# A sandwich layer on one core: the high and low halves of the non-convolution weights are kept in DRAM and loaded as pairs

## The chip, the core and the metric

The kernel runs on one core of one Trainium2 chip. Its engines work side by side and meet through semaphores: TensorE (PE) multiplies, VectorE (DVE), ScalarE (ACT) and GpSimd (POOL) work on tiles in SBUF, and SyncE (SP) issues the transfers between DRAM and SBUF. The metric is the device time in microseconds (us) of one execution; lower is better. It is given as the median of several runs.

## What is computed

The input is 4 sequences of 512 tokens with 1024 features, all in float32. Each passes through an attention block and a small mixture of experts, both wrapped in layer norms and residual sums:

```
h   = layernorm(x)
c   = conv1d(h, conv_w[3, 1024, 768], 'SAME') + conv_b        # q, k, v: 256 columns each
q,k,v = split(c);  qh = q@wq + bq;  kh = k@wk + bk;  vh = v@wv + bv   # 256 -> 16 heads of 64
p   = softmax(causal(qh @ kh.T / 8))                          # in blocks of 128 tokens
o   = (p @ vh) @ wo + bo                                      # 1024 -> 256
x1  = x + layernorm(o @ proj_w + proj_b)                      # 256 -> 1024
t   = layernorm(x1)
g   = softmax of the two largest of t @ Wr.T (4 experts), others 0
out = x1 + layernorm(sum over e of g[e] * 4 * (t @ A[e].T) @ B[e].T)   # rank 16
```

## The kernel before

**Products in two halves.** A float32 product is made of three products in a reduced float32 format: each operand is the sum of a high half (its rounded copy) and a low half (the rest), and `mm3` adds high*high, high*low and low*high. So every weight needs a high and a low copy. The weights come in 304 chunks of at most 128x512 numbers, listed in order of use in `CHUNKS`. Five kinds exist: `conv` (48 in each of the four batches), `v` (4 in a batch), `qk` (8), `wo` (8, only 256 wide) and `proj` (8, which are 4 different chunks used by two pairs of token tiles). For each chunk SP loads the float32 numbers into one of 6 slots `raw`, ACT rounds them into one of 6 slots `w_hi` (L931), and POOL or DVE subtracts to get `w_lo` (L1342, L1137). All non-convolution chunks have their low half made on POOL. The same weights are loaded and split again in every batch.

**Order of work.** The class `Plan` writes out one list of stages for all engines. Each engine's program walks the list in order and does the stages that concern it, and waits on semaphores for what it needs; so a wait holds up everything behind it on the same engine, and on SP too. Splits are planned 5 chunks ahead of their use (`LEAD`), and a load as soon as its raw slot's earlier chunk has been split, which is up to 6 chunks earlier still. A split of chunk k on ACT waits until PE has used chunk k-6, whose slot it takes.

**One batch.** The convolution comes first, in six turns of 8 chunks (a three-tap convolution done as four filters on half the tokens). In batches 1 to 3 its slots carry side work for the batch before (`SIDE`): output projection with the `proj` chunks at slots 9 to 11, layer norm 2, layer norm 3, the experts, layer norm 4 and the store of the result at slots 38 and 43. Behind each store, `load_x` brings the input of the batch after next into the same tiles `work`; it waits until the store has landed. Then come `project_v` (first half of the columns for four token tiles, then the second half), and a loop over pairs of heads: `project_qk`, `scores`, softmax, transposes, `attend`, `project_wo`. Eight convolution chunks of the next batch fill its last three rounds. `load_residual` follows the loop: the four input tiles again, 512 KB each. After batch 3 comes `TAIL`, the same side work with little to hide behind.

**Names that the prediction uses.** `work` are the four input tiles; DVE takes their statistics at L1074 and L1075 (`x_stats`), and the first layer norm needs all four. `std` is a chain of 13 small DVE instructions (L1062 to L1070), each waiting for the one before, which gives 1/standard deviation by Newton steps. `conv_out` and `conv_add` (POOL L1349, DVE L1159 and L1162) put the filters together; `project_qk` of the first pair waits for the last of them. `k_t` (DVE L1176) is the key copy that `scores` (PE L810) waits for. POOL also adds the residuals (L1362 in layer norm 2, L1368 in layer norm 4).

Of the kernel before, what the change touches and what calls it, by code (L numbers as in the profile page):

```python
# [4 lines left out]
F32 = mybir.dt.float32  # L5
I32 = mybir.dt.int32
F32R = mybir.dt.float32r
# [115 lines left out]


SUMMED = [k for k, name in enumerate(CHUNKS) if is_summed(name)]
LOADED = [k for k, name in enumerate(CHUNKS) if not is_summed(name)]

# [10 lines left out]
class Plan:  # L138
# [42 lines left out]
    def load_chunks(self):  # L181
        while self.loaded < len(CHUNKS):
            k = self.loaded
            name = CHUNKS[k]
            if not is_summed(name):
                n = LOADED.index(k)
                if n >= RAW_SLOTS and ("split", LOADED[n - RAW_SLOTS]) not in self.known:
                    break
                first = name[:2] == ("conv", 0) and name[3:] == (0, 0)
                if first and name[2] != C_ORDER[0]:  # L190
                    before = C_ORDER[C_ORDER.index(name[2]) - 1]
                    if ("sum", NUMBER["conv", 0, before, 3, HALVES - 1]) not in self.known:
                        break
                self.put("load", k)
                if first:
                    self.put("load_tap1", name[2])
            self.loaded += 1

    def split_chunks(self, upto):
# [5 lines left out]
        while self.split <= min(upto, len(CHUNKS) - 1):  # L205
# [3 lines left out]
            self.split += 1  # L209
            self.put("split", k)  # L210
            self.load_chunks()

    def use_chunk(self, *name, over=True):
# [271 lines left out]
def build(nc, x, conv_w, wq, wk, wv, wo, proj_w, biases, proj_b, aw, b_t, out):  # L485
    with ExitStack() as ctx:
# [15 lines left out]
        raw_slots = [sb(f"raw{i}", [P, CHUNK]) for i in range(RAW_SLOTS)]  # L502
        w_hi = [sb(f"w_hi{i}", [P, CHUNK], F32R) for i in range(SPLIT_SLOTS)]
        w_lo = [sb(f"w_lo{i}", [P, CHUNK], F32R) for i in range(SPLIT_SLOTS)]
        xt = [sb(f"xt{i}", [P, L + 2]) for i in range(2)]
# [51 lines left out]

        summed = nc.dram_tensor("summed_filters", (NC, 2, HALVES, P, CHUNK), F32, kind="Internal").ap()

        plan = Plan()  # L560
# [114 lines left out]
        s_tap1 = [sem(f"s_tap1_{h}") for h in range(HALVES)]  # L675
        s_small, s_lora = sem("s_small"), sem("s_lora")
        raw_full, sum_kept, work_full, stored, tap1_full = Arrival(), Arrival(), Arrival(), Arrival(), Arrival()
        for stage, *a in stages:
            if stage == "load":
                for _ in range(2 if CHUNKS[a[0]][0] == "qk" else 1):  # L680
# [32 lines left out]
        def tensor_program(pe):  # L713
# [12 lines left out]
            def use_chunk(*name):  # L726
                k = NUMBER[name]
                w.wait_ge(*split_high(k))
                w.wait_ge(*split_low(k))
                return k, w_hi[k % SPLIT_SLOTS], w_lo[k % SPLIT_SLOTS]  # L730
# [165 lines left out]
        def scalar_program(act):  # L896
# [29 lines left out]
            def split(k):  # L926
                n = width_of(k)
                if k >= SPLIT_SLOTS:
                    w.wait_ge(*chunk_used(k - SPLIT_SLOTS))
                w.wait_ge(*raw_ready(k))  # L930
                act.activation(w_hi[k % SPLIT_SLOTS][:, 0:n], raw_of(k)[:, 0:n], ACT.Copy).then_inc(*split_high.now(k))  # L931
# [446 lines left out]
        def sync_program(sp):  # L1378
# [5 lines left out]
            def tap_half(tap, c, half):  # L1384
                rows = slice(half * HALF * P, (half + 1) * HALF * P)
                return conv_w[tap, rows, c * P:(c + 1) * P].rearrange("(k p) n -> p k n", p=P)

            def load(k):
                name = CHUNKS[k]
                n = LOADED.index(k)  # L1390
                slot, full = raw_slots[n % RAW_SLOTS], s_raw[n % RAW_SLOTS]
# [63 lines left out]
            def store(b, t0):  # L1455
# [4 lines left out]
            run = {  # L1460
                "load": load, "load_tap1": load_tap1, "sum": sum_, "load_x": load_x, "load_residual": load_residual,
                "setup": setup, "store": store,
# [43 lines left out]
```

## Time and profile before

| | us |
|---|---|
| median of 3 runs | 950.44 (947.37 to 952.57) |
| the profiled execution, its own time | 947.76 |
| its span, from first to last instruction | 946.0 |
| PE, PEld busy | 776.5, 687.6 |
| DVE, POOL, ACT busy | 688.2, 526.1, 494.1 |
| mean granted clock of TensorE | 0.913 of full speed |
| bytes read, written in DRAM | 90.47 MB, 14.68 MB |

Times in the trace count from the first instruction. Batch 0 takes the first 220 us or so, the batches repeat every 218 to 219 us, and the tail begins at about 860. An engine's busy time is the sum of its instructions; PE instructions overlap, so a busy PE is not a PE at its peak. The granted clock is 1.00 at 2.4 GHz and 0.50 at 1.2 GHz.

### The profile page before, as it was taken

To read this page: it belongs to the slowest core of one execution; us is meant where nothing else is said; L and a number is where in the kernel's file an instruction comes from. 1 tells how busy PE (TensorE), PEld (TensorE's weight loads), DVE (VectorE), ACT (ScalarE), POOL (GpSimd) and SP (SyncE) were. 2 spreads that over 40 slices of the span, in tenths; PEclk is the share of its full clock that TensorE was granted. 3 is DMA by queue.
4 is the path that set the end of the run, shared out by engine and by line. 5 is a ranking of instruction groups with operands and counts; after the bars stand their busy time and mean duration, and the time that the engine had idled before them with its cause. 6 is when DMAs were issued, how large, how long until landed. Compare 5 with 4: busy or idle time off the path is not lost.

```text
span 946.0 us, 15442 instructions
## 1 busy us (share of the span) xinstructions
PE 776.5 (82%) x5136; PEld 687.6 (73%) x5136; DVE 688.2 (73%) x1796; ACT 494.1 (52%) x1156; POOL 526.1 (56%) x450
## 2 busy tenths in 40 slices
PE   2587788999949697999968887999986968997573
PEld 1487786888949685788968776788886967876472
DVE  6988777895887665987696675798597673555856
ACT  3443346875436345676536445777436445565332
POOL 2555574667673573676773564677783456444211
PEclk9889999999979897999988987999997979999856
DMA  7254662113724262212733345111743433113002
GB/s 212 74 157 129 209 208 76 40 57 98 248 68 146 80 226 85 57 45 81 247 109 106 118 149 164 45 52 51 236 143 90 125 119 125 49 53 123 1 0 89
DMA packets 108414, 106.15 MB, mean 112 GB/s; under 512 B 7600, under 2 KB 83376, under 8 KB 108336
## 3 DMA queue, kind: packets, MB, share of 16 engines
q1 hardware_dynamic: 108336, 105.18, 35.4%
q8 instruction: 41, 0.67, 0.3%
q14 instruction: 37, 0.30, 0.1%
HBM read 90.47 MB, written 14.68 MB: 111 GB/s over the span
## 4 chain that ended last, share of the span: by engine, by line
DVE 39%; PE 36%; ACT 9%; issue 9%; DMA 5%; POOL 1%; SPq 0%; DVEq 0%; ACTq 0%
PE bank L733 9%; PE bank L734 8%; PE bank L735 8%; ACT prob L981 5%; PE bank L867 3%; DVE newton L1067 3%; DVE prob_t L1200 3%; DVE filt L1097 2%; PE bank L810 2%; DVE newton L1068 2%; DVE ln_r L1069 2%; DVE ln_r L1065 2%; PE bank L829 2%; DVE prob L1184 2%; DMA work<-x 2%
## 5 line engine op out<-in xcount | busy, mean ns | idle before, releaser
L1342 POOL TENSOR_TENSOR w_lo<-raw,w_hi 128x512 fp32r<-128x512 f32 (+1 forms) x217 | 271.5, 1265 | 142.7 <-ACT w_hi L931 141.0
L733 PE MATMUL bank<-f_hi,w_hi 128*128 128x256 f32 x768 | 232.0, 302 | 40.2 <-POOL w_lo L1342 19.7
L734 PE MATMUL bank<-f_lo,w_hi 128*128 128x256 f32 x768 | 225.3, 293 | 0.0
L735 PE MATMUL bank<-f_hi,w_lo 128*128 128x256 f32 x768 | 224.8, 293 | 0.0
L931 ACT ACTIVATE w_hi<-raw 128x512 fp32r<-128x512 f32 (+1 forms) x280 | 162.0, 600 | 70.4 <-PE bank L735 59.3
L733 PEld LDWEIGHTS bank<-f_hi,w_hi 128*128 128x128 f32 x768 | 156.0, 203 | 47.2 <-ACT w_hi L931 19.1
L734 PEld LDWEIGHTS bank<-f_lo,w_hi 128*128 128x128 f32 x768 | 155.9, 203 | 0.8
L735 PEld LDWEIGHTS bank<-f_hi,w_lo 128*128 128x128 f32 x768 | 155.5, 202 | 0.0
L1353 POOL TENSOR_TENSOR prob<-prob,rtotal 128x512 f32<-128x512 f32 x64 | 84.4, 1331 | 123.4 <-DVE rtotal L1192 123.4
L981 ACT ACTIVATE prob<-prob,ntop 128x128 f32<-128x128 f32 x256 | 99.3, 390 | 36.5 <-DVE ntop L1188 36.5
L1137 DVE TENSOR_TENSOR w_lo<-raw,w_hi 128x512 fp32r<-128x512 f32 x63 | 55.9, 895 | 16.8 <-ACT w_hi L931 16.8
L733 PE MATMUL bank<-c_hi,w_hi 128*128 128x512 f32 x128 | 57.3, 448 | 8.1 <-DVE prob L1162 6.2
L810 PE MATMUL bank<-k_t,q_t 64*128 64x128 f32 x512 | 55.9, 289 | 8.3 <-DVE k_t L1176 8.2
L1184 DVE CUSTOM_DVE_ANT_0 prob<-bank,mask 128x128 f32<-128x128 f32 x256 | 58.4, 281 | 3.6 <-PE bank L810 3.5
L810 PEld LDWEIGHTS bank<-k_t,q_t 64*128 64x128 f32 x512 | 49.9, 191 | 14.9 <-issue 14.9
L860 PE MATMUL bank<-ident,v 128*128 128x128 f32 x128 | 23.0, 340 | 42.2 <-ACT v L902 42.2
L1368 POOL TENSOR_TENSOR work<-work,v 128x1024 f32<-128x1024 f32 x14 | 35.1, 2530 | 39.9 <-ACT v L902 39.7
L924 ACT ACTIVATE f_hi<-filt 128x1024 fp32r<-128x1024 f32 x28 | 29.6, 1058 | 51.1 <-POOL filt L1335 48.4
L1349 POOL TENSOR_TENSOR k_t<-q_t 128x256 f32<-128x256 f32 x48 | 38.0, 813 | 30.7 <-ACT q_t L948 26.0
L829 PE MATMUL bank<-prob_t,v 128*64 128x128 f32 x512 | 51.9, 279 | 2.9 <-DVE prob_t L1200 2.9
L1362 POOL TENSOR_TENSOR work<-work,v 128x1024 f32<-128x1024 f32 x14 | 33.8, 2433 | 34.1 <-ACT v L902 34.1
L734 PE MATMUL bank<-c_lo,w_hi 128*128 128x512 f32 x128 | 51.7, 404 | 0.0
(132 smaller groups left out, 1739.7 us busy)
## 6 DMA issues: line engine op xcount, KB each, us to landing
raw<-conv_w SPq DMA_DIRECT2D x96, 256.0 KB, 3.1
raw<-summed_filters SPq DMA_DIRECT2D x72, 256.0 KB, 2.8
work<-x SPq DMA_DIRECT2D x32, 512.0 KB, 5.6
raw<-proj_w SPq DMA_DIRECT2D x32, 256.0 KB, 2.9
out<-work SPq DMA_DIRECT2D x16, 512.0 KB, 3.8
summed_filters<-prob_t SPq DMA_DIRECT2D x16, 256.0 KB, 4.3
raw<-wv SPq DMA_DIRECT2D x16, 256.0 KB, 3.0
raw<-wq SPq DMA_DIRECT2D x32, 128.0 KB, 2.3
```

Of the source, the lines that this page charges most:

```text
L733: pe.matmul(dst, w_h, m_h, start=start, stop=False)
L734: pe.matmul(dst, w_h, m_l, start=False, stop=False)
L735: return pe.matmul(dst, w_l, m_h, start=False, stop=stop)
L810: ins = pe.matmul(score_banks[g][:, toks], q_t[rows, toks], k_t[rows, toks], start=True, stop=True)
L829: ins = pe.matmul(acc[g * DH:(g + 1) * DH, toks], v[:, t, head:head + DH], prob_t[:, g, toks], start=True, stop=True)
L931: act.activation(w_hi[k % SPLIT_SLOTS][:, 0:n], raw_of(k)[:, 0:n], ACT.Copy).then_inc(*split_high.now(k))
L981: ins = act.activation(prob[:, g, t, :], prob[:, g, t, :], ACT.Exp, bias=ntop[:, g, t:t + 1], scale=QK_SCALE, accum_out=total[:, g, t:t + 1])
L1137: dve.tensor_tensor(lo, raw_of(k)[:, 0:n], hi.bitcast(F32), ALU.subtract).then_inc(*split_low_dve.now(k))
L1184: ins = dve.tensor_tensor_reduce(prob[:, g, t, :], score_banks[g][:, t * P:(t + 1) * P], mask[:, :], 1.0, NEG_INF * 4, ALU.add, ALU.max, t ...
L1342: pool.tensor_tensor(lo, raw_of(k)[:, 0:n], hi.bitcast(F32), ALU.subtract).then_inc(*split_low_pool.now(k))
L1349: pool.tensor_tensor(m12_sums[:, i, :], m12[:, 0, :], m12[:, 1, :], op).then_inc(*m12_summed.now(b, turn, i))
L1353: pool.tensor_tensor(prob[:, g, :, :], prob[:, g, :, :], rtotal[:, g, :].rearrange("p (t o) -> p t o", o=1).broadcast_to([P, TB, P]), ALU. ...
```

## The change

The first chunk with given weights (all of batch 0's `v`, `qk` and `wo`, and the first four `proj`: 24 chunks in all, `KEPT`) is loaded and split as before, and then SP also writes its high and low half, side by side, to a DRAM tensor `kept_pairs` (stage `keep`). In batches 1 to 3 the 84 non-convolution chunks (`is_whole`) are no longer loaded as float32 and split: one transfer of both halves, 512 KB (256 KB for `wo`), goes straight into the slot `w_pair` (`load_whole`). It needs no raw slot, but it needs the slot of chunk k-6 free, so SP itself waits for the use of chunk k-6, and the load is planned when chunk k-5 is used. Raw slots now serve the convolution, batch 0 and the last four `proj` of batch 0 alone. The loads stay in one order, so a convolution load behind a whole one waits with it.

```diff
--- before.py
+++ after.py
@@ -122,8 +122,22 @@
     return name[0] == "conv" and name[1] == 0 and name[3] in (1, 2)
 
 
+def weights_of(name):
+    return name[:1] + (name[3:] if name[0] == "proj" else name[2:])
+
+
+def is_whole(k):
+    return CHUNKS[k][0] != "conv" and CHUNKS[k][1] > 0
+
+
 SUMMED = [k for k, name in enumerate(CHUNKS) if is_summed(name)]
-LOADED = [k for k, name in enumerate(CHUNKS) if not is_summed(name)]
+WHOLE = [k for k in range(len(CHUNKS)) if is_whole(k)]
+LOADED = [k for k, name in enumerate(CHUNKS) if not is_summed(name) and not is_whole(k)]
+KEPT = {}
+for k, name in enumerate(CHUNKS):
+    if name[0] != "conv":
+        KEPT.setdefault(weights_of(name), k)
+KEPT_AT = {weights: i for i, weights in enumerate(KEPT)}
 
 
 def low_on_dve(k):
@@ -182,7 +196,11 @@
         while self.loaded < len(CHUNKS):
             k = self.loaded
             name = CHUNKS[k]
-            if not is_summed(name):
+            if is_whole(k):
+                if ("used", k - SPLIT_SLOTS) not in self.known:
+                    break
+                self.put("load", k)
+            elif not is_summed(name):
                 n = LOADED.index(k)
                 if n >= RAW_SLOTS and ("split", LOADED[n - RAW_SLOTS]) not in self.known:
                     break
@@ -207,8 +225,11 @@
             if k >= SPLIT_SLOTS and ("used", k - SPLIT_SLOTS) not in self.known:
                 break
             self.split += 1
-            self.put("split", k)
+            if not is_whole(k):
+                self.put("split", k)
             self.load_chunks()
+            if k in KEPT.values():
+                self.put("keep", k)
 
     def use_chunk(self, *name, over=True):
         k = NUMBER[name]
@@ -500,8 +521,8 @@
         aw_sb = sb("aw_sb", [P, KD, ER + E])
         lora_b = [sb(f"lora_b{i}", [P, D], F32R) for i in range(2)]
         raw_slots = [sb(f"raw{i}", [P, CHUNK]) for i in range(RAW_SLOTS)]
-        w_hi = [sb(f"w_hi{i}", [P, CHUNK], F32R) for i in range(SPLIT_SLOTS)]
-        w_lo = [sb(f"w_lo{i}", [P, CHUNK], F32R) for i in range(SPLIT_SLOTS)]
+        w_pair = [sb(f"w_pair{i}", [P, 2, CHUNK], F32R) for i in range(SPLIT_SLOTS)]
+        w_hi, w_lo = [pair[:, 0, :] for pair in w_pair], [pair[:, 1, :] for pair in w_pair]
         xt = [sb(f"xt{i}", [P, L + 2]) for i in range(2)]
         filt = sb("filt", [P, FILT, L2])
         f_hi = sb("f_hi", [P, KD, FILT, L2], F32R)
@@ -556,6 +577,8 @@
         banks_of = {"stream": bank[0:2], "v": bank[2:4], "turn": bank[4:6], "side": bank[6:8]}
 
         summed = nc.dram_tensor("summed_filters", (NC, 2, HALVES, P, CHUNK), F32, kind="Internal").ap()
+
+        kept_pairs = nc.dram_tensor("kept_pairs", (len(KEPT), P, 2, CHUNK), F32, kind="Internal").ap()
 
         plan = Plan()
         stages, at = plan.stages, plan.at
@@ -674,9 +697,16 @@
         s_out = [sem(f"s_out{t}") for t in range(TB)]
         s_tap1 = [sem(f"s_tap1_{h}") for h in range(HALVES)]
         s_small, s_lora = sem("s_small"), sem("s_lora")
+        s_whole = [sem(f"s_whole{i}") for i in range(SPLIT_SLOTS)]
+        s_kept = [sem(f"s_kept{i}") for i in range(SPLIT_SLOTS)]
         raw_full, sum_kept, work_full, stored, tap1_full = Arrival(), Arrival(), Arrival(), Arrival(), Arrival()
+        whole_full, pair_kept = Arrival(), Arrival()
         for stage, *a in stages:
-            if stage == "load":
+            if stage == "load" and is_whole(a[0]):
+                whole_full.expect(s_whole[a[0] % SPLIT_SLOTS], a[0])
+            elif stage == "keep":
+                pair_kept.expect(s_kept[a[0] % SPLIT_SLOTS], a[0])
+            elif stage == "load":
                 for _ in range(2 if CHUNKS[a[0]][0] == "qk" else 1):
                     raw_full.expect(s_raw[LOADED.index(a[0]) % RAW_SLOTS], a[0])
             elif stage == "load_tap1":
@@ -725,8 +755,11 @@
 
             def use_chunk(*name):
                 k = NUMBER[name]
-                w.wait_ge(*split_high(k))
-                w.wait_ge(*split_low(k))
+                if is_whole(k):
+                    w.wait_ge(*whole_full(k))
+                else:
+                    w.wait_ge(*split_high(k))
+                    w.wait_ge(*split_low(k))
                 return k, w_hi[k % SPLIT_SLOTS], w_lo[k % SPLIT_SLOTS]
 
             def mm3(dst, w_h, w_l, m_h, m_l, start, stop):
@@ -927,6 +960,8 @@
                 n = width_of(k)
                 if k >= SPLIT_SLOTS:
                     w.wait_ge(*chunk_used(k - SPLIT_SLOTS))
+                if k - SPLIT_SLOTS in KEPT.values():
+                    w.wait_ge(*pair_kept(k - SPLIT_SLOTS))
                 w.wait_ge(*raw_ready(k))
                 act.activation(w_hi[k % SPLIT_SLOTS][:, 0:n], raw_of(k)[:, 0:n], ACT.Copy).then_inc(*split_high.now(k))
 
@@ -1385,8 +1420,24 @@
                 rows = slice(half * HALF * P, (half + 1) * HALF * P)
                 return conv_w[tap, rows, c * P:(c + 1) * P].rearrange("(k p) n -> p k n", p=P)
 
+            def load_whole(k):
+                i, n, first = k % SPLIT_SLOTS, width_of(k), KEPT[weights_of(CHUNKS[k])]
+                w.wait_ge(*chunk_used(k - SPLIT_SLOTS))
+                if k - SPLIT_SLOTS in KEPT.values():
+                    w.wait_ge(*pair_kept(k - SPLIT_SLOTS))
+                w.wait_ge(*pair_kept(first))
+                sp.dma_start(w_pair[i][:, :, 0:n].bitcast(F32), kept_pairs[KEPT_AT[weights_of(CHUNKS[k])], :, :, 0:n]).then_inc(s_whole[i], 16)
+
+            def keep(k):
+                i, n = k % SPLIT_SLOTS, width_of(k)
+                w.wait_ge(*split_high(k))
+                w.wait_ge(*split_low(k))
+                sp.dma_start(kept_pairs[KEPT_AT[weights_of(CHUNKS[k])], :, :, 0:n], w_pair[i][:, :, 0:n].bitcast(F32)).then_inc(s_kept[i], 16)
+
             def load(k):
                 name = CHUNKS[k]
+                if is_whole(k):
+                    return load_whole(k)
                 n = LOADED.index(k)
                 slot, full = raw_slots[n % RAW_SLOTS], s_raw[n % RAW_SLOTS]
                 if n >= RAW_SLOTS:
@@ -1458,7 +1509,7 @@
                     sp.dma_start(out[b * TB + t], work[t][:, :]).then_inc(s_out[t], 16)
 
             run = {
-                "load": load, "load_tap1": load_tap1, "sum": sum_, "load_x": load_x, "load_residual": load_residual,
+                "load": load, "keep": keep, "load_tap1": load_tap1, "sum": sum_, "load_x": load_x, "load_residual": load_residual,
                 "setup": setup, "store": store,
             }
             for stage, *args in stages:
```

## Rows read from the trace of the kernel before

**Rows 1.** The page, its first part: busy us, share of the span, instructions.
```profile
PE 776.5 (82%) x5136; PEld 687.6 (73%) x5136; DVE 688.2 (73%) x1796; ACT 494.1 (52%) x1156; POOL 526.1 (56%) x450
```

**Rows 2.** Stretches: us, busy PE, PEld, DVE, ACT, POOL, then clock, DMA share, GB/s.
```profile
394.50:403.43 8.93, 8.93 (x63) 7.39 (x63) 8.11 (x28) 6.70 (x23) 6.36 (x6) 1.00 0.20 59
...
474.00:548.00 74.00, 53.35 (x413) 52.29 (x412) 58.13 (x137) 34.26 (x55) 40.19 (x29) 0.87 0.35 104
```

**Rows 3.** Groups by line and shape, the two splits.
```profile
L1342 POOL TENSOR_TENSOR w_lo<-raw,w_hi 128x512 fp32r<-128x512 f32 x185 | 245.5, 1339 | 140.6 <-ACT w_hi L931 138.9
...
L931 ACT ACTIVATE w_hi<-raw 128x512 fp32r<-128x512 f32 x248 | 150.0, 625 | 70.4 <-PE bank L735 59.3 <-DMA raw<-proj_w 7.5 <-DMA raw<-wk 1.5
...
L1342 POOL TENSOR_TENSOR w_lo<-raw,w_hi 128x256 fp32r<-128x256 f32 x32 | 26.7, 837 | 2.1 <-ACT w_hi L931 2.1
```

**Rows 4.** Timeline (start, us, instruction, idle before) around batch 1's `project_v`.
```profile
347.83 0.35 PE L733 MATMUL bank<-f_hi,w_hi 128*128 128x256 f32 x1 [1.08 <-DVE w_lo L1137]
...
360.38 0.79 PE L733 MATMUL bank<-c_hi,w_hi 128*128 128x512 f32 x1 [3.66 <-DVE prob L1162]
...
367.04 1.68 PE L810 MATMUL bank<-k_t,q_t 64*128 64x128 f32 x16 [1.30 <-DVE k_t L1176]
...
341.63 5.50 POOL L1368 TENSOR_TENSOR work<-work,v 128x1024 f32<-128x1024 f32 x2 [2.56 <-ACT v L902]
...
358.26 0.69 DVE L1074 BATCH_NORM_STATS2 stats<-work 128x6 f32<-128x512 f32 x1 [8.19 <-DMA work<-x]
...
348.69 0.93 SPq L1458 DMA_DIRECT2D out<-work  x2
```

**Rows 5.** The chain that ended last, 348 to 359 (start, us, what).
```profile
348.69 3.16 DMA out<-work
351.87 6.38 DMA work<-x
```

**Rows 6.** Busy time by stretch, batch 1's `project_v` and `project_qk`.
```profile
349.30:356.60 7.30, 7.30 (x32) 5.40 (x30) 0.77 (x2) 2.34 (x4) 7.17 (x7) 1.00 1.01 332
356.60:360.30 3.70, 0.12 (x1) 0.00 (x0) 2.04 (x4) 0.00 (x0) 0.00 (x0) 0.77 0.83 268
360.30:366.00 5.70, 5.36 (x12) 3.79 (x12) 4.14 (x19) 3.60 (x7) 1.97 (x2) 0.55 0.23 69
```

**Rows 7.** Timeline, batch 3: the same place.
```profile
778.01 5.51 POOL L1368 TENSOR_TENSOR work<-work,v 128x1024 f32<-128x1024 f32 x2 [2.36 <-ACT v L902]
...
785.71 0.39 PE L733 MATMUL bank<-w_hi,c_hi 128*128 128x512 f32 x1
```

**Rows 8.** Timeline, batch 0: the same place.
```profile
135.32 1.26 SPq L1440 DMA_DIRECT2D work<-x  x1
...
140.13 0.69 DVE L1074 BATCH_NORM_STATS2 stats<-work 128x6 f32<-128x512 f32 x1 [3.64 <-DMA work<-x]
...
143.50 0.69 DVE L1074 BATCH_NORM_STATS2 stats<-work 128x6 f32<-128x512 f32 x1
...
148.93 1.23 PE L810 MATMUL bank<-k_t,q_t 64*128 64x128 f32 x12 [3.65 <-DVE k_t L1176]
```

**Rows 9.** Busy time by stretch: output projection, and residual loads alone.
```profile
446.00:476.00 30.00, 30.00 (x205) 27.55 (x206) 20.15 (x33) 14.01 (x23) 20.56 (x17) 1.00 0.77 245
...
467.00:470.00 3.00, 3.00 (x21) 2.67 (x20) 2.65 (x5) 1.90 (x3) 1.30 (x2) 1.00 1.00 362
...
864.00:867.00 3.00, 1.80 (x9) 1.51 (x10) 1.11 (x3) 3.00 (x14) 1.18 (x2) 1.00 0.99 396
```

**Rows 10.** Timeline, side work of batch 1: POOL's splits and layer norm 2.
```profile
472.56 1.21 DVE L1067 TENSOR_TENSOR newton<-ln_r 128x2 f32<-128x2 f32 x1
475.24 0.16 DVE L1067 TENSOR_TENSOR newton<-ln_r 128x2 f32<-128x2 f32 x1
...
468.69 6.30 POOL L1342 TENSOR_TENSOR w_lo<-raw,w_hi 128x512 fp32r<-128x512 f32 x5 [2.66 <-ACT w_hi L931]
...
457.43 2.25 SPq L1445 DMA_DIRECT2D work<-x  x4
```

## The prediction

> **What bounds the kernel now.** I read the page first: PE is busy for 82% of the span and every other engine for less [rows 1]. Then the busy time by stretch, to see where PE is not full. In the steady rounds of attention it is full: 8.93 of 8.93 us at clock 1.00, while ACT has 6.70 us of work and POOL 6.36 [rows 2]. So an ACT or POOL instruction taken out there is worth nothing. PE's slack lies behind the output projection: 53.35 busy in 74.00 us [rows 2], where it waits for the layer norms. Last I read the timeline and the chain at the start of the projections of batches 1 to 3, because there a store, a load and `project_v` meet. PE waits 3.66 us for the last filter sum and 1.30 us for `k_t` [rows 4], and its clock drops to 0.55 [rows 6].
>
> **What is removed.** 84 loads and splits. On POOL that is 60 x 1.339 + 24 x 0.837 = 100 us, on ACT at least 60 x 0.625 = 37 us [rows 3]. Nearly all of it runs under a full PE, so I count it as nothing there. If PE were not the cover, an attention round would be set by DVE (8.11 us), which loses no instruction.
>
> **What is added.** The 60 wide pairs carry 0.262 MB more each, the 24 narrow ones 0.131, together 18.9 MB; the 24 kept pairs are 10.5 MB of writes. At 396 GB/s [rows 9] a pair of 0.524 MB takes 1.32 us of the DMA engines. A store of that size that went out alone landed 3.16 us after its issue [rows 5], so I take 3.16 for a transfer alone and 1.32 more for each in front of it. The real question is what is late, stretch by stretch.
>
> **Batches 1 and 2, start of the projections.** Before, all loads of `v` were out long in advance. Now the load of the first `v` chunk is planned at the use of chunk k-5, which is slot 43, behind the store of tiles 2 and 3. SP waits there for POOL's residual sum, done at 341.63 + 5.50 = 347.13 [rows 4]. So: store of tile 3 at 347.2, first `v` pair at 347.6, here at 347.2 + 3.16 + 1.32 = 351.7. Then `load_x` of tile 2 needs its store landed (stored at 344.4 when the first of the two sums is done, landed 347.6), goes out at 348.0, and the second `v` pair at 348.4 lands at 351.7 + 2 x 1.32 = 354.3. Queued behind are `load_x` of tile 3 (its store lands at 350.4), the second half of `v` and the first `qk` pair, each 1.3 us apart, so 355.6 to 359.5. PE is ready for `v` at about 349.3 and does 30 products at 0.228 us [rows 6]: three at 351.7, 27 from 354.3, done at 360.5. Before, `project_qk` began at 360.38 [rows 4], because DVE stood 8.19 us for tile 2, a load issued at 351.87 behind a store issued at 348.69 [rows 4, 5]. In the new order tile 2 goes out at 348.0, nearly 4 us sooner, and the filter sums are ready before 356. So `project_qk` starts at the same time; what limited it was the input tile, and what limits it now is the `v` pair. The gain is behind it: the fourth tile's statistics and `std` no longer hold `k_t`, so the 1.30 us wait goes, and about 0.7 us of slow clock with it. I take -2 us for each. The unknown is TensorE's clock, since 4.4 us of waits now lie before 30 products instead of before 12. If these run at half speed, 30 x 0.228 = 6.8 us is added and the 2.6 us that the low clock took from 12 products returns: +2 with the gain. If the clock doesn't fall at all: -5.
>
> **Batch 3, the same place.** There is no next input, and PE goes from the convolution straight into `v` at 785.71 [rows 7]; nothing hides a late pair. POOL ends at 778.01 + 5.51 = 783.52, the store goes at 783.6, the first pair lands at 783.6 + 3.16 + 1.32 = 788.1, the second at 789.4. Three products fit between. So 27 products start at 789.4 instead of 785.71 + 0.7: +3.0 us. Bounds: +1 if the pairs do not queue, +6 if the clock falls for the products behind.
>
> **Batch 0, the same place.** Pairs of `v` are being written while the input of batch 1 comes in. The third tile's load, at 135.32, gets one kept pair in front (+1.3), the fourth two (+2.6). DVE takes the third at once when it comes (140.13, after a wait of 3.64) and the fourth at 143.50, and `k_t` keeps PE waiting 3.65 us at 148.93 [rows 8]. The fourth has about 0.7 us of slack (an estimate): +1.9 us. Bounds 0 and 2.6.
>
> **Output projection of batches 1 and 2.** Eight pairs instead of eight single chunks: 2.1 MB more in a stretch of 30 us in which the DMA engines are 77% busy, and full for its middle third, at 362 GB/s [rows 9]. 2.1 MB are 5.3 us of them, of 6.9 us free. But the 2.1 MB of residuals, issued at 457.43 [rows 10], now go out two `proj` pairs earlier, in front of the fourth pair, which then is about 1 us late; the convolution chunk behind it, loaded later and still to be split, 1 us more. Against that POOL no longer has two of the five low halves under `std`: four DVE steps take 1.21 us instead of 0.16 while POOL works [rows 10], but the three convolution splits left move into the same place, so one step is won. +2 - 1 = +1 us for each, passed on because the layer norms set this stretch. Bounds -4 (all four steps fast) and +6. In batch 0 the four `proj` pairs written cost the last loads some 4 us; layer norm work on DVE covers about that, and the 20.65 us that PE idles behind it [rows 2] cover the rest: +0.5, bounds 0 and 4.
>
> The Trainium skill (HBM Reference, its bandwidth table and the text below it) puts a core that streams alone at about 425 GB/s, and at 358 when both cores of a pair do. By the second figure a pair would take 1.46 us (an estimate from that page), the sum grows by under 2 us. The trace agrees with the first: 396 GB/s in long rows.
>
> **Elsewhere.** In the attention rounds a pair is asked for five chunks ahead, which is over two rounds of 8.93 us: covered. In the tail the `proj` pairs are there before the last head is done: nothing.
>
> **Sum.** +1.9 + 0.5 - 2 - 2 + 1 + 1 + 3.0 = +3.4 us on the profiled execution's own 947.76, so 951.2. That execution lies 2.7 us under the median of the runs shown, 950.44; on the median the sum gives 953.8. I take 953.0, nearer to the median.
>
> **Rivals.** *Relief counts (faster).* POOL's two-input work holds DVE up: 1.21 against 0.16 us. If four steps are freed in both output projections (-8) and the clock stays up in front of `project_qk` (-10), with batches 0 and 3 as above (+5.4), it is -13: about 938. With half of that, 944. It decides when at least two steps a batch are freed and the `v` pairs land before 353. The Trainium skill (GPSIMD Engine Reference, Specifications) says that GpSimd shares its SBUF interfaces with VectorE; the slow steps agree with that. Against: the slow steps lie under convolution splits, which stay.
> *Late pairs (slower).* In the output projection the DMA engines are already full where the pairs come. If each pair costs its 1.32 us on PE's path from the fourth on, that is +6 in each of two, +2 in batches 1 and 2, +6 in batch 3 and +6 in batch 0: +28, about 979; half of it, 965, is likelier. For it: SP now stops at the store. Against: 6.9 us of free DMA time.
> *No effect.* PE-bound and all transfers hidden: 950. It isn't told apart from my forecast by time.
>
> **How the numbers follow.** My forecast, with no effect in it, has a chance of 0.43, relief 0.27, late pairs 0.30. A change under 0.5% (4.8 us) can't be told from none. 953.0 is +0.3%. For its own case the range is 947 to 957; relief reaches to 938 and late pairs to 979, and leaving a tenth at each end gives 941 to 969. Faster by more than 0.5% is the larger part of relief and nothing else, 0.27; slower takes late pairs, 0.30, and the top of my case, 0.02, from the same, 0.41.
>
> **What would show it.** In the profile after: POOL some 100 us and ACT 40 to 50 us less busy; about 135 MB moved; attention rounds still 8.9 us; PE waiting for transfers of pairs at the start of `project_v` in batches 1 to 3, for 2 to 5 us each; `load_x` of tile 2 issued within 1 us of POOL's last sum; DMA share of 0.9 or more in the output projection. I am wrong if PE waits for pairs in attention, if the low clock covers more stretches than before, or if `std` in layer norm 2 runs through without a step over 1 us.

## The result, and the profile after

The kernel became slower: 978.36 us median of 4 runs (977.12 to 981.14), against 948.90 (947.20 to 952.57) for the kernel before in the same rounds. The ratio is 1.032, 95% interval 1.0297 to 1.0343. The profiled execution spans 976.0 us, before 946.0. The time lies outside the ranges around the forecast of 953.0 (947 to 957 for its own case, 941 to 969 with the rivals); the rival "late pairs", with 979, comes nearest.

The page of the kernel after: busy us of each engine, bytes, and the transfers (KB each, us from issue to landing).

```profile
span 976.0 us, 15110 instructions
PE 781.1 (80%) x5136; PEld 691.9 (71%) x5136; DVE 685.0 (70%) x1796; ACT 454.6 (47%) x1072; POOL 430.7 (44%) x366
...
DMA packets 106364, 135.50 MB, mean 139 GB/s; under 512 B 7600, under 2 KB 76208, under 8 KB 106288
...
w_pair<-kept_pairs SPq DMA_DIRECT2D x60, 512.0 KB, 4.6
```

Against [rows 1], POOL has 95.4 us less work (526.1 to 430.7) and ACT 39.5 us less. So the change does what it says, and none of it shortens the time. PE is busy 781.1 us instead of 776.5 with the same 5136 products, and its mean granted clock is 0.903 instead of 0.913; it stands for the rest of the span, 194.9 us instead of 169.5. So 25.4 of the 30.0 us are standing.

**Where the 30 us are.** I take three marks on PE in every batch: the first `scores` (S), the first turn of the experts' input (T), and the turn behind the gates of the second pair of token tiles (M). S to T holds the attention rounds, the output projection and the layer norms in front of the experts; M to S the end of the convolution, the store, `project_v` and the first `project_qk`. All times in us, from one profiled execution of each kernel; "to S, batch 0" counts from the first instruction. The marks are read to about 0.1 us.

| stretch | before | after | forecast of the difference | measured |
|---|---|---|---|---|
| to S, batch 0 | 148.9 | 153.0 | +1.9 | +4.1 |
| S to M behind batch 0's attention | 180.4 | 181.6 | +0.5 | +1.2 |
| M to S, start of batch 1's attention | 37.7 | 37.3 | -2 | -0.4 |
| S to M, batch 1's output projection in it | 180.5 | 190.9 | +1 | +10.4 |
| M to S, batch 2's | 36.8 | 37.6 | -2 | +0.8 |
| S to M, batch 2's output projection in it | 181.3 | 190.9 | +1 | +9.6 |
| M to S, batch 3's | 31.2 | 35.5 | +3.0 | +4.3 |
| behind S of batch 3, the tail in it | 149.2 | 149.2 | 0 | 0.0 |

The measured column adds up to 30.0, the difference of the spans. Two thirds of it are in the output projections of batches 1 and 2.

**What happens there.** The timeline of batch 1's output projection in the kernel after, engine by engine (start, us, instruction, and in brackets the idle time before it with what ended it):

```profile
455.68 3.14 SPq L1429 DMA_DIRECT2D w_pair<-kept_pairs  x3
458.88 2.25 SPq L1496 DMA_DIRECT2D work<-x  x4
461.22 0.61 SPq L1429 DMA_DIRECT2D w_pair<-kept_pairs  x1
461.93 0.81 SPq L1456 DMA_DIRECT2D raw<-conv_w  x1
...
471.80 0.63 ACT L966 ACTIVATE w_pair<-raw 128x512 fp32r<-128x512 f32 x1 [11.28 <-DMA raw<-conv_w]
...
472.46 0.69 DVE L1172 TENSOR_TENSOR w_pair<-raw,w_pair 128x512 fp32r<-128x512 f32 x1 [9.91 <-ACT w_pair L966]
473.07 0.68 DVE L1254 TENSOR_TENSOR v<-bank,projb 128x512 f32<-128x512 f32 x1
...
473.81 0.79 PE L766 MATMUL bank<-w_pair,po_hi 128*128 128x512 f32 x1 [8.33 <-DVE v L1254]
...
702.14 0.80 PE L766 MATMUL bank<-w_pair,po_hi 128*128 128x512 f32 x1 [8.49 <-DVE v L1254]
```

Read it from the end. PE stands 8.33 us because DVE has not emptied a bank of the output projection (`proj_bias`, L1254). DVE is idle, though; it walks its list in order, and in front of that instruction stands the low half (L1172) of a convolution chunk, slot 10 of the next batch. For that DVE needs ACT's high half, and ACT stands 11.28 us for the chunk itself. The load of the chunk went out at 461.93 and was there at 471.7. The last row is the same place in batch 2. The chain that ended last goes the same way (start, us, what):

```profile
461.93 9.78 DMA raw<-conv_w
...
471.80 0.64 ACT w_pair L966
...
473.07 0.70 DVE v L1254
...
473.81 0.79 PE bank L766
```

Why a chunk of 256 KB takes 9.78 us is seen in SP's waits between 446 and 470 (us in total, times, longest), and in the busy time by stretch (columns as in [rows 2]):

```profile
SPq L1429 <- PE bank L768: 12.2, 4, 9.1
```

```profile
446.00:450.00 4.00, 3.14 (x22) 2.58 (x21) 1.81 (x3) 1.00 (x2) 1.46 (x2) 1.00 0.95 311
450.00:453.00 3.00, 3.00 (x29) 2.83 (x28) 1.04 (x3) 1.60 (x4) 1.27 (x1) 1.00 0.04 12
453.00:456.00 3.00, 3.00 (x22) 2.72 (x21) 0.40 (x1) 1.45 (x3) 2.29 (x2) 1.00 0.00 0
...
465.00:468.00 3.00, 0.48 (x3) 0.05 (x1) 0.00 (x0) 0.00 (x0) 0.00 (x0) 1.00 1.03 416
468.00:471.00 3.00, 0.00 (x0) 0.00 (x0) 0.00 (x0) 0.00 (x0) 0.00 (x0) 0.74 1.06 383
471.00:474.00 3.00, 0.19 (x1) 0.20 (x2) 1.51 (x3) 0.63 (x1) 0.00 (x0) 0.50 0.83 301
474.00:477.00 3.00, 3.00 (x8) 2.32 (x9) 2.63 (x5) 1.15 (x2) 0.00 (x0) 0.50 0.04 11
477.00:480.00 3.00, 3.00 (x12) 2.52 (x11) 1.83 (x3) 0.00 (x0) 0.00 (x0) 0.56 0.32 106
...
455.68:471.71 16.03, 9.80 (x72) 8.94 (x70) 2.38 (x4) 1.87 (x3) 2.04 (x3) 0.93 0.89 319
```

From 450 to 455.7 nothing moves (share 0.04 and 0.00). SP stands at the load of a pair, which may not go before PE has used chunk k-6; one such wait is 9.1 us long. Then three pairs, the four residuals, one more pair and the chunk go out within 7 us. They are 4.5 MB; with the first part of two more pairs behind them the DMA engines move 5.1 MB in the 16.03 us until the chunk is there, at 319 GB/s.

From 465.5 to 473.8 PE does nothing, and then it works at clock 0.50 (1.2 GHz) until about 479.7. A product starts every 0.43 us there, later every 0.23, so the 5.9 us of work at the low clock cost some 2.7 us (an estimate from these rows). The stall and this make 11.0, a little more than the 10.4 of the table, because the kernel before has a low clock elsewhere in the stretch (0.50 from 368.9 to 372.2, right behind S, where this kernel has 1.00). Over S to T as a whole PE stands 24.9 us instead of 15.1 and is busy 119.2 instead of 118.5.

**The start of the projections** in batch 1, SP and PE:

```profile
349.51 3.15 SPq L1509 DMA_DIRECT2D out<-work  x2
352.76 0.38 SPq L1429 DMA_DIRECT2D w_pair<-kept_pairs  x1
353.18 0.78 SPq L1491 DMA_DIRECT2D work<-x  x1
354.06 0.41 SPq L1429 DMA_DIRECT2D w_pair<-kept_pairs  x1
...
357.41 0.77 PE L766 MATMUL bank<-w_pair,c_hi 128*128 128x512 f32 x1 [2.78 <-issue]
359.92 0.80 PE L766 MATMUL bank<-w_pair,c_hi 128*128 128x512 f32 x1 [0.89 <-DMA w_pair<-kept_pairs]
...
371.88 1.68 PE L843 MATMUL bank<-k_t,q_t 64*128 64x128 f32 x16 [0.93 <-DVE k_t L1211]
```

Everything is about 5 us later than in [rows 4], since batch 0 has cost that much. The order is as forecast: the store, the first `v` pair, the input tile 0.4 us behind it, the second pair. PE waits for the pairs, and the 3.66 us before `project_qk` are gone. (The profile names no releaser for the 2.78 us; they are gone where `v` is loaded as before, in a run below.) But the stretch is as long as before: 2.78 and 0.89 us are as much as the 3.66, `k_t` still keeps PE for 0.93 us where it was 1.30, and the clock falls to 0.50 for 6.8 us in both kernels, here behind 356.8 and before behind 358.6.

### The profile page after: what moved, and what is told of

It reads as the page before. It is cut to its first block, busy times and chain, and to the rows that moved or that the text cites. A ratio compares the mean times of both kernels' runs of the same rounds, so it can differ in the third digit from the quotient of the medians.

```text
span 976.0 us, 15110 instructions
## 1 busy us (share of the span) xinstructions
PE 781.1 (80%) x5136; PEld 691.9 (71%) x5136; DVE 685.0 (70%) x1796; ACT 454.6 (47%) x1072; POOL 430.7 (44%) x366
## 4 chain that ended last, share of the span: by engine, by line
PE 40%; DVE 34%; issue 8%; DMA 7%; ACT 7%; SPq 2%; POOL 2%; ACTq 0%; DVEq 0%; POOLq 0%
PE bank L766 10%; PE bank L768 9%; PE bank L767 9%; ACT prob L1016 3%; PE bank L843 3%; PE bank L862 3%; PE bank L900 3%; DVE newton L1102 3%; DVE ln_r L1104 2%; DVE newton L1103 2%; DMA raw<-conv_w 2%; DVE ln_r L1100 2%; DVE prob_t L1235 2%; PE bank L893 2%; DVE stats L1321 2%
## 5 line engine op out<-in xcount | busy, mean ns | idle before, releaser
L766 PE MATMUL bank<-f_hi,w_pair 128*128 128x256 f32 x768 | 231.6, 302 | 37.5 <-POOL w_pair L1377 17.5
L1377 POOL TENSOR_TENSOR w_pair<-raw,w_pair 128x512 fp32r<-128x512 f32 (+1 forms) x133 | 172.9, 1312 | 168.6 <-ACT w_pair L966 167.6
L767 PE MATMUL bank<-f_lo,w_pair 128*128 128x256 f32 x768 | 225.1, 293 | 0.0
L768 PE MATMUL bank<-f_hi,w_pair 128*128 128x256 f32 x768 | 224.9, 293 | 0.0
L766 PEld LDWEIGHTS bank<-f_hi,w_pair 128*128 128x128 f32 x768 | 156.0, 203 | 44.4 <-issue 16.5
L966 ACT ACTIVATE w_pair<-raw 128x512 fp32r<-128x512 f32 (+1 forms) x196 | 116.6, 615 | 97.3 <-PE bank L768 38.2
L767 PEld LDWEIGHTS bank<-f_lo,w_pair 128*128 128x128 f32 x768 | 155.8, 203 | 1.0
L768 PEld LDWEIGHTS bank<-f_hi,w_pair 128*128 128x128 f32 x768 | 155.3, 202 | 0.0
L1172 DVE TENSOR_TENSOR w_pair<-raw,w_pair 128x512 fp32r<-128x512 f32 x63 | 54.3, 869 | 40.7 <-ACT w_pair L966 40.7
L766 PE MATMUL bank<-c_hi,w_pair 128*128 128x512 f32 x128 | 54.7, 427 | 4.5 <-DVE prob L1197 2.7
L893 PEld LDWEIGHTS bank<-ident,v 128*128 128x128 f32 x128 | 19.4, 181 | 43.7 <-ACT v L935 43.7
```

Source lines behind the costliest of these rows:

```text
L766: pe.matmul(dst, w_h, m_h, start=start, stop=False)
L767: pe.matmul(dst, w_h, m_l, start=False, stop=False)
L768: return pe.matmul(dst, w_l, m_h, start=False, stop=stop)
L893: ins = pe.transpose(dst[:, i * P:(i + 1) * P], y[t][:, kt * P:(kt + 1) * P], ident[:, :])
L1172: dve.tensor_tensor(lo, raw_of(k)[:, 0:n], hi.bitcast(F32), ALU.subtract).then_inc(*split_low_dve.now(k))
L1377: pool.tensor_tensor(lo, raw_of(k)[:, 0:n], hi.bitcast(F32), ALU.subtract).then_inc(*split_low_pool.now(k))
```

## The experiments

Twelve kernels were run, each compared with the kernel before in the same rounds. None of them leaves out a part of the computation. The stretches come from one profiled execution of each.

### All pairs but those of the output projection

```diff
-    return CHUNKS[k][0] != "conv" and CHUNKS[k][1] > 0
+    return CHUNKS[k][0] in ('v', 'qk', 'wo') and CHUNKS[k][1] > 0
...
-    if name[0] != "conv":
+    if name[0] in ('v', 'qk', 'wo'):
```

> The changed kernel with the proj chunks loaded and split as before; v, qk and wo stay kept pairs. Theory A (the loss sits in the output projection, where the pairs and the 2 MB of residual loads stand in one queue in front of convolution chunk 158, whose low half on DVE stands in front of the bias additions): the two waits of 8.3 and 8.5 us and the slow clock behind them go, 978 - 25 = 953 us. Theory B (each of the 84 pairs costs about the same wherever it is loaded): 24 of 84 pairs gone is 0.3 of 30 us, 969 us. Theory C (the writes and the first stretches of batch 0 cost most): above 970 us.

Measured: 953.14 us (951.36 to 955.25), ratio 1.0052 (1.0034 to 1.0071), as theory A expected. S to T in batches 1 and 2 takes 131.4 and 131.6 us: not only are the 10 us gone, both are 2 us shorter than before (133.6, 134.0). M to S of batch 3 keeps its extra, 36.8.

### The pairs of the output projection alone

The same two lines with `('proj',)`.

> The opposite: only the proj chunks are kept pairs. Theory A: before + 25, 974 us, with the same two waits of PE of about 8 us at the second half of the output projection. Theory B: before + 9, 958 us. Theory C: under 955 us, for only four pairs are written, and late in batch 0.

Measured: 971.95 us (970.61 to 972.62), ratio 1.0242 (1.0214 to 1.0269), near the 974 of theory A. Its PE rows:

```profile
473.81 0.80 PE L766 MATMUL bank<-w_pair,po_hi 128*128 128x512 f32 x1 [8.56 <-DVE v L1254]
...
701.70 0.80 PE L766 MATMUL bank<-w_pair,po_hi 128*128 128x512 f32 x1 [8.30 <-DVE v L1254]
```

The two halves of the change cost 4.4 and 23.2 us over the kernel before; together 27.6 of the 29.5 of the whole. So the large loss belongs to these eight pairs a batch, whatever the other weights do.

### The residual loads sooner

The four `load_residual` of batches 0 to 2 move from behind the loop over the heads to the start of its round 8 (the ninth), ahead of the pairs of the output projection.

```diff
             for i in range(HP + LAG):
+                if more and i == HP:
+                    for t in range(TB):
+                        put("load_residual", b, t)
...
             put("finish_wo", b)
-            for t in range(TB):
-                put("load_residual", b, t)
+            if not more:
+                for t in range(TB):
+                    put("load_residual", b, t)
```

> The changed kernel; the residual loads of batches 0 to 2 go out one stage earlier, at the start of the ninth round of attention, when the DMA engines stand still, instead of behind the last round. Nothing else is changed. Theory A: chunk 158 no longer stands behind 2.1 MB, it comes 5 us or more earlier, PE's waits of 8.3 and 8.5 us fall under 3, and the clock stays up: 978 - 20 = 958 us. Theory B (the pairs are late in themselves, 2.1 MB more in a full stretch): the waits keep over 5 us each, 972 us or more.

Measured: 962.13 us (961.34 to 962.21), ratio 1.0138 (1.0116 to 1.0159): 16 us of the 29.5 are back, where theory A had 20. S to M is 8.7 and 6.8 us shorter than in the kernel after in batches 1 and 2, so nearly all of it is there. In the timeline the convolution chunk now stands right behind the four pairs, and ACT begins on it 5.2 us after its issue. PE's wait for `proj_bias` is 2.04 us, in batch 2 2.5 us:

```profile
453.81 4.56 SPq L1433 DMA_DIRECT2D w_pair<-kept_pairs  x4
458.46 0.39 SPq L1460 DMA_DIRECT2D raw<-conv_w  x1
...
463.64 0.63 ACT L970 ACTIVATE w_pair<-raw 128x512 fp32r<-128x512 f32 x1 [4.99 <-PE bank L772]
...
465.65 0.50 PE L770 MATMUL bank<-w_pair,po_hi 128*128 128x512 f32 x1 [2.04 <-DVE v L1258]
```

2.1 MB in front of the chunk, at the 416 GB/s of the stretch above, are 5 us. So most of the wait was one for the queue and not for the transfer of that chunk. The same edit also gives 7 us without any pairs (below); how much of the 16 us is that gain was not taken apart.

### The low halves of slots 10 and 11 on POOL

```diff
-LOW_ON_DVE = {5, 7, 10, 11, 16,
+LOW_ON_DVE = {5, 7, 16,
```

> The changed kernel; the low halves of slots 10 and 11 (chunks 158 and 161 and their like in batches 1 to 3) are made on POOL instead of DVE. Theory A with DVE's order as the whole cause: the bias additions no longer wait for chunk 158, PE goes on to project the second half, and the 8 us fall to 3 or less in each of two batches: about 964 us. Theory A with the late load as the cause: PE goes on for 2.8 us and then waits for chunk 158 itself, 3 us less in each: about 971 us. If the fourth proj pair is what PE waits for, nothing changes: 978 us.

Measured: 972.42 us (970.11 to 975.22), ratio 1.0249 (1.0219 to 1.0279), 6 us less than the kernel after. Nothing stands in front of `proj_bias` now, and the wait shrinks from 8.33 and 8.49 us to these:

```profile
470.88 0.55 PE L766 MATMUL bank<-w_pair,po_hi 128*128 128x512 f32 x1 [4.36 <-DMA w_pair<-kept_pairs]
...
694.62 0.80 PE L766 MATMUL bank<-w_pair,po_hi 128*128 128x512 f32 x1 [4.85 <-DMA w_pair<-kept_pairs]
```

So about half of the stall was the order on DVE, and the other half is there without it: the fourth pair itself is late, behind the residuals. That is the cause of the third case expected, which had put the time at 978, with no gain; the time is near the 971 of the second, whose cause (PE waiting for the chunk) does not appear. S to M is 5.3 and 3.7 us shorter than in the kernel after in batches 1 and 2, but M to S of batches 1 and 3 is some 2 us longer. The way through DVE is shown, and so is its limit.

### The residual loads sooner in the kernel before

The edit of the residual loads, in the kernel without pairs.

> The kernel before, with nothing kept, and the residual loads of batches 0 to 2 at the start of the ninth round of attention as in the run of that name. Theory: before the change PE never waited in the output projection, so there is nothing to win: 948 us, within 2 us. Rival: the full queue already cost there (ACT waits 7.5 us for proj loads), 944 us or less.

Measured: 940.82 us (940.14 to 941.93), ratio 0.993 (0.9904 to 0.9956). I had expected no change; the rival was right in time. The gain is spread: 2.6 us in M to S of batch 1, about 1 each in S to T of batches 0 and 2 and in M to S of batch 3. It is not in the output projection of batch 1, where PE is as full as before. And it is not a wait that is gone: over the span PE stands 173.1 us, before 169.5, but is busy 766.6 us with the same 5136 products, before 776.5. M to S of batch 1, before and with the edit (columns as in [rows 2]):

```profile
329.30:367.00 37.70, 31.67 (x172) 27.34 (x172) 22.16 (x54) 16.49 (x29) 20.78 (x16) 0.84 0.58 195
```

```profile
328.70:363.80 35.10, 28.97 (x172) 25.49 (x173) 22.17 (x54) 16.41 (x29) 20.81 (x16) 0.93 0.63 210
```

PE stands 6.0 and 6.1 us; what differs is the granted clock, 0.84 and 0.93. So in these two executions the gain is a higher clock. Why it is higher stays open, and one of the four runs, at a mean clock of 0.912, took 941.93 us all the same, while the kernel before had 0.909 to 0.917 in these rounds.

### All pairs but those of `v`

The two lines with `('qk', 'wo', 'proj')`.

> The changed kernel with the v chunks loaded and split as before; qk, wo and proj stay kept pairs. Theory: at the start of the projections the v pair, whose load stands behind the store on SP, is what PE waits for, and the input tile that used to hold PE now comes early. Without v pairs both waits are gone: batch 3 gains 4.4 us, batches 1 and 2 some 4 us each, batch 0 (four pairs less to write) 2 us: 964 us, with no wait of PE over 1.5 us between the last convolution chunk and the first scores. Rival (the earlier load of the input tile came from the splits that are gone, and is lost with v's splits back): batches 1 and 2 fall back by 2 us each, 976 us.

Measured: 958.45 us (956.54 to 959.08), ratio 1.0114 (1.0091 to 1.0137), more of a gain than expected (964). M to S falls to 31.8 and 31.6 us in batches 1 and 2, from 37.3 and 37.6, and to 31.2 in batch 3. In batch 1 PE stands 2.8 us instead of 5.7 and is busy 29.0 instead of 31.6, so half of the gain is waits and half is clock (0.92 instead of 0.84). The stalls of the output projection are still there, 8.55 and 8.30 us. SP around the store of batch 1:

```profile
348.12 3.15 SPq L1509 DMA_DIRECT2D out<-work  x2
351.31 2.84 SPq L1491 DMA_DIRECT2D work<-x  x2
354.26 5.44 SPq L1429 DMA_DIRECT2D w_pair<-kept_pairs  x4
```

`v` was loaded long before, as single chunks, and the input tiles go out in front of all pairs. So, with the other kinds as pairs, the pairs of `v` cost 5.5 and 6.0 us in batches 1 and 2 (I had this place as a gain of 2) and 4.3 in batch 3.

### The last store later

In front of batch 3 the store of tiles 2 and 3 comes four slots after its place instead of one.

```diff
-            self.later(STORE_LAG, lambda: self.put("store", b, t0))
+            self.later(4 if (b, t0) == (2, 2) else STORE_LAG, lambda: self.put("store", b, t0))
```

> The changed kernel; in the convolution of batch 3 alone the second store of batch 2's result is planned three slots later, so that the loads of the v pairs go out in front of it and not behind it. Theory: SP's stop at the store is what makes the pair late; PE's wait of 2.95 us at batch 3's v goes, with the slow clock behind it 3 to 4 us in all: 974 us. Rival (the pair is late by the time it takes): the wait stays, 978 us.

Measured: 972.70 us (972.02 to 975.13), ratio 1.0272 (1.0247 to 1.0297), near the 974 expected. M to S of batch 3 is 31.0 instead of 35.5; all else is within 1.1 us of the kernel after. The profile had put that wait down to DVE (2.95 us, `prob` L1197), but it goes when only the order of the store and the pairs changes.

### The writes alone

`is_whole` returns `False`: the 24 pairs are written in batch 0 and never read.

> The 24 pairs are written to DRAM in batch 0, and nothing is read back: batches 1 to 3 load and split as before. This prices the writes. Theory: they hold up the input tiles of batch 1, batch 0 is 4 us longer (PE's first scores at about 152 instead of 149 us, and 1 us in the output projection), and nothing else changes: 953 us. Rival (hidden): 949 us. Rival (the rest of batch 0's 5.3 us is the writes in the output projection): over 955 us.

Measured: 951.35 us (949.07 to 953.59), ratio 1.0047 (1.0028 to 1.0067). That is 2.7 to 6.4 us over the kernel before; the median lies between the 953 expected and the 949 of "hidden", nearer to the first. In its profiled execution batch 0's S is at 153.3, where the kernel after has 153.0. But this mark moves without any writes too: in the four kernels that write no pair in front of it, it lies at 148.9 (the kernel before), 149.8, 151.2 and 152.5. So the median prices the writes, and a single timeline does not.

### Pairs of `qk` and `wo` alone

The two lines with `('qk', 'wo')`: what the runs so far left of the change.

> Kept pairs for qk and wo alone: v and proj are loaded and split as before. The stretches of the earlier runs should add up. From scores to scores: with v split as before the start of the projections is 5.9 and 5.1 us shorter than before the change (batches 1 and 2), with proj split as before attention and output projection are 2.1 and 2.5 us shorter, batch 0 gets nothing from writes of v. Theory: 948 - 15 = 933 us. Rival (the gains belong to v and proj pairs, which are gone here): 948 us, as before.

Measured: 932.84 us (931.72 to 934.57), ratio 0.9847 (0.9818 to 0.9876). It is as expected and beats both kernels. M to S is 32.0 and 30.6 us in batches 1 and 2, and S to T is 1.6 and 2.7 us shorter than before. Its SP, to be read against [rows 4, 5]:

```profile
346.18 3.15 SPq L1509 DMA_DIRECT2D out<-work  x2
349.38 2.84 SPq L1491 DMA_DIRECT2D work<-x  x2
352.32 5.45 SPq L1429 DMA_DIRECT2D w_pair<-kept_pairs  x4
```

The input tile is asked for at 349.38, before at 351.87 (though M of batch 0 is 1.7 us later here), and `project_qk` need not wait 3.66 us for the sums behind it. Over the span PE stands 165.8 us instead of 169.5, and is busy 765.5 instead of 776.5 with the same products. So most of this gain too is clock: the waits that are gone are the smaller part of it.

### Pairs of `qk` and `wo`, and the residual loads sooner

> The same with the residual loads of batches 0 to 2 at the start of the ninth round of attention. In the kernel before that gave 7 us. Theory: some of it is in the same waits that the qk pairs have removed, so 2 to 5 us are left: 929 to 931 us. Rival (independent, the full 7 us): 926 us.

Measured: 928.97 us (927.59 to 931.74), ratio 0.9814 (0.9779 to 0.9849). It is as expected and the fastest version of this study, though its slowest run (931.74) touches the fastest of the one above (931.72).

### The store sooner in the kernel before

Is the gain of that version only the earlier store? In the kernel before, the store of tiles 2 and 3 of batches 0 and 1 is put in the plan at once, ahead of the `qk` loads.

```diff
-            self.later(STORE_LAG, lambda: self.put("store", b, t0))
+            if (b, t0) in ((0, 2), (1, 2)):
+                self.put("store", b, t0)
+            else:
+                self.later(STORE_LAG, lambda: self.put("store", b, t0))
```

> The kernel before, with no kept pair; in the convolutions of batches 1 and 2 the second store is planned one slot sooner, in front of the load of the qk chunk that on SP waits for the last split. Theory (the pairs of qk gain at the start of the projections because SP gets sooner to the store and so to the input tile behind it): PE's wait of 3.7 us before project_qk shrinks by 3 us in batch 1 and 2 us in batch 2, with the slow clock behind it 942 us. Rival (the gain comes from the splits that are gone from ACT and POOL): no change, 948 us.

Measured: 941.75 us (940.23 to 948.31, 10 runs), ratio 0.9943 (0.9922 to 0.9964), as expected. M to S: 33.7 and 34.5 us, against 37.7 and 36.8. So part of the gain is a matter of order and needs no pairs. The input tile went out at 354.57, still behind loads of `qk`.

### Pairs of `qk` alone

> Kept pairs for qk alone. Theory (the gain is SP's: the loads behind the last convolution chunks that stop it at a split are those of qk): nearly all of the gain of qk and wo together, within 3 us of that run, 934 to 936 us. Rival (the gain is in the number of splits taken off POOL and ACT, 24 of 48 here): half of it, 941 us.

Measured: 937.31 us (935.50 to 938.24), ratio 0.989 (0.9861 to 0.9919). It lies between what was expected and the rival's 941. M to S is nearly as short as with `wo` (31.4, 32.4), so these 10.9 us under the kernel before are the pairs of `qk`, and the other 4.5 come with those of `wo`, in S to T of batch 2 above all (134.2 against 131.3). There PE stands 14.8 us here and 15.5 with the pairs of `wo`, but is busy 119.4 and 115.8 with the same products, at clock 0.95 and 0.97: again clock and not a wait. Why was not taken apart.

## Why the prediction was wrong, step by step

- **What is removed is worth nothing under a full PE:** right. From 372 to 446 PE is busy 71.71 us at clock 1.00, before 71.77; POOL has 39.45 us of work there instead of 52.45.
- **Output projection of batches 1 and 2, the step that failed: the cost of late loads, taken as +1 each.** The prediction said "2.1 MB are 5.3 us of them, of 6.9 us free", "about 1 us late; the convolution chunk behind it [...] 1 us more", and so +1 each. Measured: +10.4 and +9.6. Two things in it were wrong. The free time of the DMA engines was an average over 30 us, but the change itself moves the start of every load: 5.7 us of it lie before 455.7, when SP may not issue. (What this stop costs by itself no run shows.) And the late chunk was priced at its own use, but it is waited for sooner: its low half is made on DVE, in front of the instruction that empties PE's banks. The fourth pair was taken to be 1 us late; without the low half in front PE waits 4.4 and 4.9 us for it. The same pairs without the other weights cost 23.2 us; with the residuals out of the way 16 us come back; without the low half on DVE half of each stall stays. So the queue behind SP's stop is shown as the cause, with two ways to PE, one through DVE and one through the fourth pair.
- **Start of batches 1 and 2, -2 each:** the waits came as described (5.1 us later, the store, the pairs and the input tile go out within 0.6 us of the times forecast), the gain did not: -0.4 and +0.8. The step that failed here is "the 1.30 us wait goes, and about 0.7 us of slow clock with it": in batch 1 `k_t` keeps PE for 0.93 us and the low clock lasts 6.8 us as before. In batch 2 PE stands 5.7 us instead of 6.0 and is busy 31.9 instead of 30.8. Taking the pairs of `v` out gives 5.5 and 6.0 us; the larger effect, which the prediction did not look at, was that the pairs of `qk` free the input tile when `v` stays outside.
- **Start of batch 3, +3.0:** right in mechanism, +4.3 measured and removed by moving the store. PE stands 4.8 us instead of 1.8, the +3.0; the rest is that it is busy 30.7 instead of 29.4, which was named as a bound.
- **Batch 0, +1.9 and +0.5:** +4.1 and +1.2 in this execution; the writes alone cost 3.5 us between the medians of the same rounds. In the timeline DVE's wait for the third input tile has grown from 3.64 [rows 8] to 7.10 us, with one kept pair written in front of its load:

```profile
136.54 0.47 SPq L1435 DMA_DIRECT2D kept_pairs<-w_pair  x1
137.05 1.06 SPq L1491 DMA_DIRECT2D work<-x  x1
...
144.19 0.69 DVE L1109 BATCH_NORM_STATS2 stats<-work 128x6 f32<-128x512 f32 x1 [7.10 <-DMA work<-x]
```

  But the same wait is 5.41 us in the kernel before with the store sooner, which writes no pair, and S is at 152.5 there. Some 1.2 us of the 4.1 are there at 121 us, before any pair is written. So whether +1.9 was too little is not shown.
- **Relief in layer norm 2:** it did not come. Before, three steps of `std` took 1.21 us and one 0.77, now four take 1.21 to 1.28, beside 0.16; POOL makes four low halves of the convolution from 485.33 to 490.40:

```profile
487.95 1.21 DVE L1102 TENSOR_TENSOR newton<-ln_r 128x2 f32<-128x2 f32 x1
...
490.64 0.16 DVE L1102 TENSOR_TENSOR newton<-ln_r 128x2 f32<-128x2 f32 x1
```

- **Tail, 0:** 149.2 and 149.2.
- **Late pairs, 979:** right in size, and in place for the output projection, but its working had each pair cost 1.32 us on PE's path. It is one convolution chunk that is late, in batches 1 and 2, with 8.4 us of standing and some 2.7 us of low clock behind it. That the sum fits is in part luck: its terms were +12 for the two output projections (measured 20.0), +4 for the starts of batches 1 and 2 (0.4), +6 for batch 3 (4.3) and +6 for batch 0 (5.3).

One sign of being wrong that the prediction named was a low clock in more stretches than before; that agrees with the mean granted clock, 0.903 instead of 0.913.

What stays open: why the clock is higher when the residual loads go sooner (7 us in the kernel before), and when `wo` comes as pairs (4.5).

## What to carry to other kernels

A load that needs no staging buffer needs its final buffer instead, so it can go only when that is free; with one in-order queue everything behind it starts as late, and free bandwidth before that moment is lost. When a transfer may be late, follow not only who uses its data but which instructions stand behind the first one that waits for it, on each engine: here an 0.7 us subtraction held up the evacuation of PSUM, and with it PE. And try a change on each kind of data by itself: the same edit gave 15 us for two kinds of weights and cost 23 for another. Compare the busy time of the same products too, and not only the waits: 776.5 and 765.5 us in two of these kernels.

## What the hardware showed that I had not expected

Pairs and residuals together, behind each other in one queue, moved at 416 GB/s with a share of 1.03 (465 to 468), more than the 396 GB/s of [rows 9]. After 8.3 us without work TensorE worked at 0.50 from 473.8 to about 479.7, so each such stop cost more than its own length. And moving the four residual loads of each batch, in the kernel before, left PE's waits as long as they were while its products took 9.9 us less.
